# A causal attention layer beside a recurrence on one core: scores of four heads at once in four PSUM banks, transposes in the dense banks, recurrence steps spaced by work

## The reference, cut to what matters

```python
# x: (8, 512, 512); 16 heads of 32; image_hidden_states = h0 = cond (8, 512)
qkv = x @ c_attn_w + c_attn_b                      # q, k, v of the 512 words
k = concat([img @ uk_w.T + uk_b, k]);  v = concat([img @ uv_w.T + uv_b, v])
scores = q @ k.T / sqrt(32)                        # per batch element and head, causal
attn = softmax(where(causal, scores, -10000) + mask)
x = x + (attn @ v) @ c_proj_w + c_proj_b           # layer 0
xw = x @ Wx + b
for t in range(512):                               # layer 1: 512 steps, one after the other
    h = tanh(h @ Wh + xw[:, t])
    hs[:, t] = h
return x + hs
```

## Time and profile before

| what | value |
|---|---|
| three timed runs | 1696.03, 1696.64, 1708.65 us; median 1696.64 us |
| the profiled execution | 1703.19 us, span 1701.4 us |
| PE busy | 1613.0 us (95% of the span) |
| weight loads busy | 1254.3 us (74%) |
| DVE busy | 792.6 us (47%) |
| ACT busy | 661.7 us (39%) |
| POOL busy | 185.6 us (11%) |
| granted TensorE clock, mean | 0.981 of full speed |

### The profile page before, as it was taken

The page is one execution under the profiler, slowest core; times in us unless marked ns, Lnnn a source line. Parts: engine busy times, 40 slices in busy tenths (PEclk is TensorE's granted clock), DMA queues, the critical chain, the costliest instruction groups (busy, mean ns, idle before and its releaser), DMA issues.

```text
span 1701.4 us, 74131 instructions
## 1 busy us (share of the span) xinstructions
PE 1613.0 (95%) x32749; PEld 1254.3 (74%) x32749; DVE 792.6 (47%) x2687; ACT 661.7 (39%) x2257; POOL 185.6 (11%) x300
## 2 busy tenths in 40 slices
PE   7889999999999999999999999999999999999775
PEld 6667777777777878777777877777777777777554
DVE  3444444454445454454545555454554554554221
ACT  3434333433334443443444444444434444443111
POOL 2111111111011010111011010110101111000000
PEclk9869999999999999999999999999999999999999
DMA  6322111222223122332323323233332443321000
GB/s 232 87 50 70 42 54 52 69 65 61 56 59 92 57 83 67 85 83 69 83 62 110 103 83 90 65 115 97 91 86 72 124 111 99 93 71 34 15 9 15
DMA packets 167903, 130.24 MB, mean 77 GB/s; under 512 B 54264, under 2 KB 153112, under 8 KB 167072
## 3 DMA queue, kind: packets, MB, share of 16 engines
q1 hardware_dynamic: 153792, 92.92, 19.3%
q0 software_dynamic: 13792, 32.58, 6.8%
HBM read 100.00 MB, written 25.43 MB: 74 GB/s over the span
## 4 chain that ended last, share of the span: by engine, by line
PE 88%; issue 3%; ACT 3%; DVE 2%; DMA 2%; SPq 1%; POOL 0%; DVEq 0%; ACTq 0%; POOLq 0%
PE rec L1047 26%; PE turned L977 11%; PE scores L966 9%; PE dense L495 8%; PE dense L496 7%; PE dense L497 7%; PE rec L1038 6%; PE pv L994 5%; PE pv L1012 2%; PE scores L1047 2%; DVE pre L873 1%; ACT states L727 1%; PE dense L948 1%; PE dense L1054 1%; DMA xin<-x 1%
## 5 line engine op out<-in xcount | busy, mean ns | idle before, releaser
L1047 PE MATMUL rec<-wh,states 128*32 128x128 f32 x15360 | 516.9, 275 | 28.8 <-ACT states L727 27.4
L1047 PEld LDWEIGHTS rec<-wh,states 128*32 128x32 f32 x15360 | 400.1, 110 | 125.3 <-ACT states L727 67.9
L679 ACT ACTIVATE probs<-probs,nmax 128x64 f32<-128x64 f32 (+7 forms) x512 | 270.6, 529 | 250.0 <-DVE nmax L818 247.5
L873 DVE STREAM_TRANSPOSE pre<-rec 128x128 f32<-128x128 f32 x480 | 151.8, 316 | 450.6 <-PE rec L1047 449.0
L727 ACT ACTIVATE states<-pre 128x32 f32<-128x32 f32 x512 | 133.0, 260 | 450.8 <-DVE pre L873 448.9
L818 DVE CUSTOM_DVE_ANT_0 probs<-scores,msk,nimg 128x64 f32<-128x64 f32 (+7 forms) x512 | 245.6, 514 | 38.8 <-PE scores L966 31.6
L977 PE MATMUL turned<-ident,probs 128*128 128x128 f32 (+1 forms) x1280 | 242.4, 291 | 8.7 <-ACT probsT L686 8.0
L977 PEld LDWEIGHTS turned<-ident,probs 128*128 128x128 f32 (+1 forms) x1280 | 132.4, 135 | 82.9 <-issue 68.6
L966 PE MATMUL scores<-kt,q 32*64 32x64 f32 (+7 forms) x2048 | 186.1, 431 | 0.3 <-DVE nmax L818 0.2
L827 DVE COPY probsT<-turned 128x128 f32<-128x128 f32 (+3 forms) x256 | 124.9, 488 | 77.1 <-PE turned L977 71.7
L495 PE MATMUL dense<-xT_hi,wqkv_hi 128*128 128x256 f32 x488 | 150.9, 309 | 1.4 <-DVE xT_lo L775 1.4
(11 more groups left out here) (148 smaller groups left out, 1779.9 us busy)
## 6 DMA issues: line engine op xcount, KB each, us to landing
vbuf<-v_dram SPq DMA_DIRECT2D x64, 192.0 KB, 2.8
xin<-x SPq DMA_DIRECT2D x64, 128.0 KB, 3.0
v_dram<-vbuf POOLq DMA_DIRECT2D x64, 128.0 KB, 2.7
out<-outs POOLq DMA_DIRECT2D x32, 256.0 KB, 4.2
vbuf<-v_dram SPq DMA_DIRECT2D x64, 128.0 KB, 2.4
kt<-k_dram SPq DMA_DIRECT2D x16, 512.0 KB, 4.1
vbuf<-v_dram SPq DMA_DIRECT2D x32, 256.0 KB, 3.3
k_dram<-knew POOLq DMA_DIRECT2D x60, 128.0 KB, 2.6
```

Of the source, the lines that this page charges most:

```text
L679: act.activation(probs[:, g % PROBS, 0:n], probs[:, g % PROBS, 0:n], ACT.Exp, scale=-1.0, bias=nmax[:, e, h:h + 1], accum_out=rowsum[:, e, ...
L873: dve.transpose(pre_all, rec_bank(g // GROUP)[:, 0:P]).then_inc(pre_ready, 1)
L1047: last = pe.matmul(rec_bank(g // GROUP)[Q * j:Q * j + Q, 0:P], state_tile(g - 1)[:, f, :], wh[:, f, P * j:P * j + P], start=False, stop=f ...
```

## The change

1. **Four banks of scores.** `scores` has `HC` = 4 banks. The scores of four head units are issued together, one in each bank and each from another group of 32 rows of the array, once per four head units; before, two together, once per two.
2. **No banks of their own for transposes.** `turned0` and `turned1` are gone. A `turn` is now one more job in the rotation over the dense banks: two banks while the recurrence runs (`dense0`, `dense1`), three before it. It waits for the copy of whatever used its bank last, and the next dense product waits for its copy.
3. **Maxima and exponentials apart from the scores.** A new kind `softmax` stands in the list for DVE's and ACT's part; of four head units the first comes at head unit u, the second and third at u+1, the fourth at u+2.
4. **Steps by work.** The 448 steps are spread over the whole stretch from the end of the second trip to the last trip's projection, in proportion to the weights, and not 32 to each trip. A step is never set before its block is finished, nor between two of the four scores. The order now holds 22, 26, 30, 29, 31, 31, 34, 35, 35, 36, 38, 37, 42 and 22 steps from projection to projection, where it held 32 each.
5. `vfirst` and `v` of one product follow each other at once in the list; `turn` copies only the partitions that it wrote; weights of the scores in the planner are new; set-up uses the four score banks where it used two and two.

```diff
-            if u % 2 == 0:
-                emit([("score", v, 0, 0.07 + 0.107 * keys(g) / P) for v in (u, u + 1)])
+            if u % HC == 0:
+                emit([("score", v, 0, 0.06 + 0.06 * keys(g) / P) for v in range(u, u + HC)])
+            emit([("softmax", v, 0, 0.0) for v in ((u,), (u, u + 1), (u + 1,), ())[u % HC]])
...
+            if out[-1][0] == "vfirst":
+                share -= side[0][3]
+                emit([side.pop(0)])
...
-    for b in range(PARTS - 1):
-        first = ends[(b + 1) * QUADS - 1] + 1
-        for n in range(QUADS):
-            last = begins[(b + 1) * QUADS + n]
-            whole = sum(w for *_, w in main[first:last])
-            done, t = 0.0, 0
-            for at in range(first, last):
-                done += main[at][3]
-                if main[at][0] == "score" and main[at][1] % 2 == 0:
-                    continue
-                while t < STEPS and (done >= whole * (t + 0.5) / STEPS or at + 1 == last):
-                    place.setdefault(at, []).append(b * W + n * STEPS + t)
-                    t += 1
-            first = last
+    first, last = ends[QUADS - 1] + 1, begins[TRIPS - 1]
+    whole = sum(w for *_, w in main[first:last])
+    done, t = 0.0, 0
+    for at in range(first, last):
+        done += main[at][3]
+        if main[at][0] == "score" and main[at][1] % HC < HC - 1:
+            continue
+        while (t < FIRST and at > ends[(t // W + 1) * QUADS - 1]
+               and (done >= whole * (t + 0.5) / FIRST or at + 1 == last)):
+            place.setdefault(at, []).append(t)
+            t += 1
...
-        if kind in DENSE_KINDS and kind != "v":
+        if kind in DENSE_KINDS + ("turn",) and kind != "v":
...
-        scores = [ctx.enter_context(nc.psum_tensor(f"scores{i}", [P, BANK], F32)) for i in range(2)]
-        turned = [ctx.enter_context(nc.psum_tensor(f"turned{i}", [P, BANK], F32)) for i in range(2)]
+        scores = [ctx.enter_context(nc.psum_tensor(f"scores{i}", [P, BANK], F32)) for i in range(HC)]
...
-                    act.copy(probsT[:, g % TURNED, 0:n], turned[1][:, 0:n]).then_inc(turned_copied[1], 1)
+                    act.copy(probsT[rows, g % TURNED, 0:n], bank(kind, g, 0)[rows, 0:n]).then_inc(copied(kind, g, 0), 1)
...
-                    dve.tensor_copy(probsT[:, g % TURNED, 0:n], turned[0][:, 0:n]).then_inc(turned_copied[0], 1)
+                    dve.tensor_copy(probsT[rows, g % TURNED, 0:n], bank(kind, g, 0)[rows, 0:n]).then_inc(copied(kind, g, 0), 1)
...
-                    if g > 1:
-                        pe.wait_ge(shifted_ready, g - 1)
+                    if g == 0:
+                        pe.wait_ge(image_ready, 1)
+                    if g >= HC:
+                        pe.wait_ge(shifted_ready, g - HC + 1)
...
-                    if g > 1:
-                        pe.wait_ge(turned_copied[g % 2], g // 2)
+                    wait_bank(pe, kind, g, 0)
...
-                    for parity in range(2):
-                        pe.wait_ge(turned_copied[parity], 2 * g + 2)
+                    for held, count in turns_copied(g).items():
+                        pe.wait_ge(dense_copied[held], count)
```

More of the change, by code:

```diff
@@ L60 @@
 LAGS = {
-    "DVE": {"xsplit": 0.7, "k": 0.2, "v": 0.2, "imgscore": 0.2, "score": 0.2, "turn": 0.2, "imgprob": 0.0,
+    "DVE": {"xsplit": 0.7, "k": 0.2, "v": 0.2, "imgscore": 0.2, "softmax": 0.2, "turn": 0.2, "imgprob": 0.0,
             "total": 0.5, "norm": 0.2, "attnlow": 0.9, "proj": 0.2, "step": 0.1, "hist": 0.8,
             "vimg": 0.2, "wproj": 0.8},
-    "ACT": {"xsplit": 0.0, "q": 0.2, "score": 0.8, "turn": 0.2, "imgprob": 0.2, "imgturn": 0.2,
+    "ACT": {"xsplit": 0.0, "q": 0.2, "softmax": 0.8, "turn": 0.2, "imgprob": 0.2, "imgturn": 0.2,
             "rowturn": 0.2, "norm": 0.6, "step": 0.5, "out": 0.2, "wproj": 0.0},
@@ L417, in attention_recurrence @@
         turned_ready = sem("turned_ready")
-        turned_copied = [sem(f"turned_copied{i}") for i in range(2)]
         pv_done = sem("pv_done")
@@ L462, in wait_copied, with turns_copied @@
             eng.wait_ge(dense_copied[n], before + 1)
+        def turns_copied(group):
+            return dict((JOB["turn", g, 0][0], JOB["turn", g, 0][1] + 1) for g in range(HC * group, HC * group + HC))
         def heads_tile(group):
@@ L652, in _ @@
                 high_qkv(i)
-            for f, d in enumerate(scores + turned):
+            for f, d in enumerate(scores):
                 act.wait_ge(setup_turned, C + 2 + f)
@@ L673, in _ @@
                                    bias=bqk[:, 0, i:i + 1]).then_inc(copied(kind, g, i), 1)
-                elif kind == "score":
+                elif kind == "softmax":
                     trip, u = divmod(g, UNITS)
@@ L682, in _ @@
                     n = P * tiles_of(g // UNITS)
+                    rows = slice(0, min(P, keys(g // UNITS)))
                     act.wait_ge(turned_ready, g + 1)
@@ L778, in _ @@
                     dve.wait_ge(setup_product, 2)
-                    dve.tensor_tensor(vimg_all, turned[0][:, :], uvb, ALU.add).then_inc(image_ready, 1)
+                    dve.tensor_tensor(vimg_all, scores[0][:, :], uvb, ALU.add).then_inc(image_ready, 1)
                     dve.wait_ge(image_ready, 1)
@@ L817, in _ @@
                         wait_copied(dve, "imgscore", trip, h // HC)
-                    dve.tensor_tensor_reduce(out=probs[:, g % PROBS, 0:n], in0=scores[g % 2][:, 0:n],
+                    dve.tensor_tensor_reduce(out=probs[:, g % PROBS, 0:n], in0=scores[g % HC][:, 0:n],
                                              in1=msk[:, e, 0:n], scale=-SCALE, scalar=nimg[:, trip % 2, e, h:h + 1],
@@ L936, in _ @@
                     for f in range(C):
-                        last = pe.matmul(turned[0][:, :], rbc[:, f, :], wh[:, f, :], start=f == 0, stop=f == C - 1)
+                        last = pe.matmul(scores[0][:, :], rbc[:, f, :], wh[:, f, :], start=f == 0, stop=f == C - 1)
                     last.then_inc(setup_product, 1)
@@ L965, in _ @@
                         at = W * (2 * e + b)
-                        last = pe.matmul(scores[g % 2][W * b:W * b + W, 0:n], q[rows, trip % 2, c, at:at + W],
+                        last = pe.matmul(scores[g % HC][W * b:W * b + W, 0:n], q[rows, trip % 2, c, at:at + W],
                                          heads_tile(group)[rows, b, :], start=True, stop=True, skip_group_check=True)
@@ L971, in _ @@
                     pe.wait_ge(probs_ready, g + 1)
-                    if g == 0:
-                        pe.wait_ge(image_ready, 1)
-                    if g > 1:
-                        pe.wait_ge(turned_copied[g % 2], g // 2)
+                    wait_bank(pe, kind, g, 0)
                     for at in range(0, n, P):
-                        last = pe.transpose(turned[g % 2][0:min(P, n - at), at:at + P],
+                        last = pe.transpose(bank(kind, g, 0)[0:min(P, n - at), at:at + P],
                                             probs[:, g % PROBS, at:min(at + P, n)], ident[:])
```

## The result

The changed kernel took 1682.33 us, median of 4 runs (1681.49 to 1685.94), beside 1700.1 us for the kernel before on the same chip. The ratio is 0.9889, 95% interval 0.9856 to 0.9922: 1.1% faster, 19 us. Timed again later (e11) it gave 0.9901 (0.9868 to 0.9935). The forecast was 2.5% faster, 42.5 us; the time lies in the upper part of the stated range. One of the four runs of e7, 3539.71 us, is left out of the ratios as a slow run.

What follows compares the result with a forecast made beforehand. PE's queue was taken to bound the trips. Scores -63.5, modes -4, banks +22 and steps +3 gave -42.5 us on the profiled 1703.2, 1660.7; as a median 1654, rounded to 1655 us, range 1630 to 1698.

Steps and rivals of the forecast that it cites:

- What bounds the kernel: In the 16 trips, a microsecond of PE's queue is a microsecond of the kernel; the last 64 steps count at nothing.
- The scores: On PE, a run of four costs one pair's time plus 0.15 us, in place of two pairs: 63.5 us saved.
- The low bound: Price of eight more score records taken as nothing, their issue hidden behind the streaming: 82.7 us saved.
- The first rival: Score runs: the four row groups don't run side by side, a run takes two pairs' time; 1696 us, chance 0.12.
- The banks: Transposes sharing two dense banks make PE wait for copies: 22 us lost, bounds 5 and 60.
- The second rival: The two shared banks become the bound: 276 jobs wait 0.4 us each, 110 us; 1735 us, chance 0.11.
- The bound of 60 us: Upper bound of the shared banks' cost, if every fourth of 146 jobs also meets a copy as late as ACT's.
- The steps: More places with too little other work between two steps of the recurrence: 3 us lost, bounds -6 and +15.
- The third rival: The spreading of the steps is the gain, waits for states vanish altogether: 1638 us, chance 0.10.
- Changes of mode: On PE, 150 fewer places where neighbours use different tile shapes, 22 counted at 0.18 us: 4 us saved, bounds 0 and 8.
- The sum: All terms together: -63.5 - 4 + 22 + 3 = -42.5 us against the profiled execution, giving 1660.7 us.
- The signs that I named: Next start 1.0 to 1.1 us after 448-key runs; `probsT` waits 15 to 30; state waits within 5 of 10.4; last stretch 139.

Runs made afterwards that it cites:

- e11: The changed kernel itself, unchanged, timed again on the same chip beside the kernel before: ratio 0.9901.
- e7: The changed kernel with the planned lags of `softmax` at 0.5 on DVE and 1.1 on ACT, for 0.2 and 0.8: ratio 0.9869.
- e3: The kernel before with only the transposes put into the rotation of the two dense banks, two banks left unused: 1749.45 us, ratio 1.0283.
- e9: The kernel before with transposes and dense products in one rotation over three banks: 1702.57 us, ratio 0.9998.
- e1: The changed kernel with the old placement of the steps, 32 to each trip: 1689.33 us, ratio 0.9935.
- e2: The kernel before with only the new placement of the steps by work: 1714.12 us, ratio 1.0061.

## Why the prediction was wrong, point by point

**What bounds the kernel** was right. PE's queue sets the time in the trips, and the stretch after them stayed at 139 us.

**The scores** were right in mechanism and too small in size. The size that was wrong is "I take 0.15 us, near `pv`": eight more records cost 0.02 to 0.03 us, not 0.15. The term was 63.5 us and measured 79.4. The low bound, where the issue hides behind the streaming, was the right end. The Trainium skill, "TensorE: Matmul & The Clock Gate", section "Measured speedup vs the span model", adds about 4 ns for each further tile, an estimate of 0.03 us for the eight. This trace agrees, with 0.026. The first rival, row groups that don't run side by side, is refuted by the same rows.

**The banks** were the largest error and the step that failed. I wrote "(28 + 8 - 4) x 2/3 = 21 us, I take 22". e3 measures 48 us. In the changed kernel 46.9 us stand behind the short kinds, though, as said above, not all of that is the banks'. Three things in that step were too kind. It took 0.75 us from a product's end to its copy's end, though the earlier trace rows show one of 1.97 us, and it left that to the upper bound. So it took no account of the queue ahead of a copy: `nimg` is copied in 0.16 us, but in the 14 waits for it, 7.7 us in all, the copy began 0.2 to 2.0 us after the image scores' end. It charged 0.10 us to distances of 0.5 to 1.0 us and nothing to longer ones, where such waits were up to 1.21 us at 0.6 us of distance and 0.56 and 0.63 us at 1.6. And the third taken off for neighbouring waits had no row behind it. The second rival had the mechanism, with a price of 110 us; the truth is between it and the forecast. The bound of 60 us held.

The Trainium skill, "Perfetto Trace Analysis", section "Matmuls" under "Optimizing Tensor Performance", wants independent groups to rotate through different banks so that the copy of one overlaps the next. The runs agree where two banks are left, which cost 48 us (e3). With three the copies were covered (e9).

**The steps** had the right sign and too small a size, for a reason that I had missed. I had +3 us; PE's waits for states and for the bias rose by 6.3 us from 170 to 1545 us, from 10.4 and 3.6 to 15.5 and 4.8. (The steps' row in the table, 453.7 and 453.4 us, says nothing of it, since a wait for a state is counted with the kind before the step.) I compared the short places of the two orders as they are, and so did not see that the new scores with the old placement would have had 13 us more of these waits (25.2 and 8.1 in e1) and taken 6 to 8 us longer. The spreading pays that back. The third rival, that the spreading is the gain, fell with the waits for states: they rose, and alone the spreading loses 10 us (e2).

**Changes of mode**, 4 us, can't be told apart in the result.

**The sum** as it came out: -79.4 (scores) + 8.8 (waiting behind score runs) + 46.9 (after transposes, image scores and outputs) + 6.2 (the rest) = -17.5 us, for 17.3 measured. As forecast: -63.5 - 4 + 22 + 3 = -42.5. The forecast was 25 us off. The scores gave 16 us more than I took. The short kinds cost 25 us more than the 22. And the two small terms, 8.8 and 6.2, stand where I had 3 - 4 = -1, 16 us more: the waits for states and bias are in part of these, in part of the 46.9, and the lower clock of this execution may be some 5 us. How the rest of the 6.2 us arose stays open.

The signs that I named came out so: the next start after a run at 448 keys 0.94 us later, below even the 1.0 to 1.1 that I gave; waits for copies of `probsT` 21.6 us, inside the 15 to 30, but with another 11.8 us for `nimg` and `outs`, which I had not named; waits for states 15.5, just outside "within 5 us of 10.4"; the last stretch 139 us, as named. So the sign that was to show the bank term right held while the term was not half of the cost: waits for `probsT` alone were too narrow a sign.

## What to carry to other kernels

When a change takes accumulation banks from short jobs to give them to long ones, count the rotation that is left before the gain: here three banks shared by transposes and dense products were free and two cost 48 us, and a run of three scores (48 us faster than before) beat a run of four (19 us faster). Charge a wait on a saturated engine from start to start, not by its idle time, and take the copy's time with its queue, not alone. A placement that helps one version can hurt another: the same spreading of the steps was worth 6 to 10 us with short scores and cost 10 us with long ones, so each part has to be tried in the company it will have. And before a difference of some microseconds between two kernels is explained, their granted clocks should be compared.

## What the runs showed of the hardware that I had not expected

- Eight matmul streams in eight parts of the array (four groups of 32 rows, two of 64 columns) run at the pace of four: 16 records at 512 keys in 1.05 us from start to start, 8 records in 1.02 us. Eight more records cost 3 ns each; the 64 records of a `pv` take 14 ns each in all.
- A short wait costs more than it shows: at 1030 us 0.49 us were lost where the row has 0.41. Over the trips, the idle time behind transposes, image scores and outputs grew by 39.4 us, and these groups, from start to start, by 46.9 us.
- Runs of one kernel differ by their granted clock: over 58 runs of the kernel before, between 0.974 and 0.988, 0.01 less goes with 9 us more of 1703.
